# Attention of a two-layer token tower: value products in runs of eight, exponents in twelve buffers, maxima turned with 128 columns

## The reference

```python
# per sequence, 512 tokens, 12 heads of width 16
q, k, v = split(h_in @ w1)                       # h_in: normalised, scaled and masked rows of 192
s = softmax(q @ k.T / sqrt(16))                  # 512 x 512 per head
attn = s @ v                                     # 512 x 16 per head
out = concat(gelu(mlp part), attn) @ w2 + b2
```

## Time and profile before

| | before |
|---|---|
| median of 3 runs | 2166.76 us (2166.21 to 2169.19) |
| span of the profiled execution, first to last instruction | 2137.2 us |
| median of the runs less that span | 29.6 us |
| TensorE busy | 1949.3 us, 91% |
| VectorE busy | 1140.4 us, 53% |
| ScalarE busy | 739.9 us, 35% |
| mean granted TensorE clock | 0.938 |
| first score to last score of the eight turns | 357.86 us to 898.84 us |

### The profile page before, as it was taken

How to read it: one execution, slowest core, us unless ns; L and a number is a source line. 1 busy time by engine, 2 the same in 40 slices (tenths; PEclk the granted TensorE clock), 3 DMA queues, 4 the chain that set the end, 5 groups by cost and what they waited for, 6 DMA issues and landing times. The chain is left out here.

```text
span 2137.2 us, 28059 instructions
## 1 busy us (share of the span) xinstructions
PE 1949.3 (91%) x10067; PEld 1227.5 (57%) x10075; DVE 1140.4 (53%) x2776; ACT 739.9 (35%) x1248; POOL 426.2 (20%) x567
## 2 busy tenths in 40 slices
PE   4998629999999999879999998799999999999997
PEld 2343523344444544445666665465558888888886
DVE  5798567676667665456877785347322222222221
ACT  1434102544555455544556553121111111111111
POOL 5200111120222021111111111100551222222222
PEclk9988558999999999978999999699999999999999
DMA  2610002111111111000000000200222322122321
GB/s 63 223 50 0 0 18 81 53 52 53 45 53 53 52 45 52 1 31 6 6 6 6 11 6 1 100 1 1 77 95 61 69 60 59 32 62 61 69 38 18
DMA packets 68748, 94.75 MB, mean 44 GB/s; under 512 B 15386, under 2 KB 57662, under 8 KB 66337
## 3 DMA queue, kind: packets, MB, share of 16 engines
q1 hardware_dynamic: 52482, 77.19, 11.2%
q0 software_dynamic: 16128, 15.76, 4.3%
HBM read 54.96 MB, written 39.47 MB: 44 GB/s over the span
## 5 line engine op out<-in xcount | busy, mean ns | idle before, releaser
L1020 DVE TENSOR_REDUCE row_max<-c_ps_m 128x1 f32<-128x512 f32 x384 | 253.1, 686 | 113.8 <-PE c_ps_m L1190 108.5
L1368 ACT ACTIVATE e<-c_ps_s 128x512 f32<-128x512 f32 x384 | 216.5, 596 | 222.2 <-PE c_ps_s L1206 221.5
L2667 DVE TENSOR_TENSOR e_f<-e_ps_u,e_gate 128x512 f32<-128x512 f32 x120 | 83.0, 692 | 271.2 <-ACT e_gate L2949 179.1
L2468 POOL DMA_INDIRECT out<-m_o,m_row_of x80 | 125.7, 1571 | 282.0 <-issue 252.9
L2884 PE MATMUL e_ps_o<-m_w,e_f 128*128 128x192 f32 x960 | 162.6, 326 | 0.9 <-DVE e_f L2667 0.9
L1190 PE MATMUL c_ps_m<-c_kT,qT 96*128 96x512 bf16 x384 | 150.4, 398 | 10.7 <-DVE row_max L1020 10.0
L2884 PEld LDWEIGHTS e_ps_o<-m_w,e_f 128*128 128x128 f32 x960 | 158.1, 190 | 3.3 <-DVE e_f L2667 1.3
L1206 PE MATMUL c_ps_s<-qT,c_kT 97*128 97x512 bf16 x384 | 145.2, 389 | 12.7 <-ACT e L1368 5.3
L2949 ACT ACTIVATE e_gate<-e_ps_g 128x512 f32<-128x512 f32 x120 | 71.6, 597 | 242.3 <-PE e_ps_g L2858 162.3
L2852 PE MATMUL e_ps_g<-m_xT,m_w 128*128 128x256 f32 x480 | 129.6, 392 | 1.0 <-DVE h L2499 1.0
L2852 PE MATMUL e_ps_u<-m_xT,m_w 128*128 128x256 f32 x480 | 123.2, 379 | 0.0
(11 more groups left out here) (458 smaller groups left out, 3725.2 us busy)
## 6 DMA issues: line engine op xcount, KB each, us to landing
dealt<-x SPq DMA_DIRECT2D x8, 1290.0 KB, 15.1
m_x<-dealt SPq DMA_DIRECT2D x40, 258.0 KB, 2.7
spread<-parts SPq DMA_DIRECT2D x24, 384.0 KB, 2.3
qT<-spread SPq DMA_DIRECT2D x144, 64.0 KB, 2.4
c_kT<-spread SPq DMA_DIRECT2D x144, 64.0 KB, 2.5
m_w<-in_w13e SPq DMA_DIRECT2D x8, 1152.0 KB, 5.2
m_w<-in_w2e SPq DMA_DIRECT2D x8, 576.0 KB, 6.2
out<-h SPq DMA_DIRECT2D x8, 384.0 KB, 4.6
```

Source lines behind the costliest of these rows:

```text
L1020: dve.tensor_reduce(row_max[:, n // J, n % J:n % J + 1], ps_m[:, n % 2, :], AX_X, ALU.max)\
L1368: act.activation(e[:, n % LIVE_E, :], ps_s[:, n % 2, :], ACT.Exp, scale=QSCALE).then_inc(e_ready, 1)
L2468: pool.indirect_dma_start(out=out_rows, out_offset=bass.IndirectOffsetOnAxis(ap=row_of[:, n % 2, r:r + 1], axis=0), in_=o[:, n % 2, r, :], ...
L2667: dve.tensor_tensor(fe[:, n % 2, 2 * i:2 * i + 2, :], ps_ue[:, q % 2], gate_e[:, q % 2], ALU.mult)\
```

## The change

Two groups are weighed in one run, in steps 9, 17, 25, 33, 41 and (the last two) behind the first MLP tile of `between`; the exponents have 12 buffers, so that eight of them can wait while four are written. `neg_max` has 128 columns per group, 16 filled and 112 zero, and the turned maxima are a 128 x 128 matmul; its first 16 rows are read as before. `xaT` moves into memory of a weight that is no longer needed, to make room.

```diff
-LIVE_E = 8
+LIVE_E = 12
...
-        neg_max = sb("neg_max", [P, HEADS, J])
+        neg_max = sb("neg_max", [P, G3, P])
...
-        xaT = sb("xaT", [CH, 2, T])
+        xaT = moe.w2_other[0:CH, :, :].rearrange("p m c -> p (m c)")[:, 0:2 * T].rearrange("p (c t) -> p c t", c=2)
...
-                dve.tensor_scalar(neg_max[:, 4 * g:4 * g + 4, :], row_max[:, 4 * g:4 * g + 4, :], -1.0, None,
-                                  ALU.mult).then_inc(mx_ready, 1)
+                dve.tensor_scalar(neg_max[:, g, 0:GS].rearrange("p (h j) -> p h j", j=J), row_max[:, 4 * g:4 * g + 4, :],
+                                  -1.0, None, ALU.mult).then_inc(mx_ready, 1)
...
+            dve.memset(neg_max[:, :, GS:P], 0.0)
...
-                pe.transpose(bank(key)[0:4 * J, 0:P], neg_max[:, 4 * g:4 * g + 4, :], kit.ident[:, :])\
-                  .then_inc(w_psum, 1)
+                pe.transpose(bank(key)[:, 0:P], neg_max[:, g, :], kit.ident[:, :]).then_inc(w_psum, 1)
...
                 mlp_tile(t, 0)
+                weigh(t - 1, G3 * J - 2)
                 weigh(t - 1, G3 * J - 1)
...
-                    if n % 4 == 1 and n > 4:
+                    if n % 8 == 1 and n > 8:
+                        weigh(t, n // 4 - 2)
                         weigh(t, n // 4 - 1)
...
+            weigh(B - 1, G3 * J - 2)
             weigh(B - 1, G3 * J - 1)
...
-                if n % 4 == 0 and t * G3 * J + n // 4 >= 2:
-                    act.wait_ge(av_done, t * G3 * J + n // 4 - 1)
+                if n % 4 == 0 and t * G3 * J + n // 4 >= LIVE_E // 4:
+                    act.wait_ge(av_done, t * G3 * J + n // 4 - LIVE_E // 4 + 1)
```

## The result

The change takes 2189.07 us (4 runs, 2186.2 to 2191.03) against 2166.49 us for before: ratio 1.0097, 95% interval 1.0069 to 1.0124. Before itself had medians of 2166.49, 2182.64, 2176.24 and 2178.52 us in the four comparisons, so a time is only set against the before of its own comparison.

A forecast was written before the change was run, and what follows sets the result against it. TensorE was taken to bound most of a turn, VectorE or ScalarE two stretches (steps 13 to 17, 28 to 33). Moved weighs +8.2 and clock +3.1 gave +11.3 us: 2148.5 span plus 29.6, 2178.0 us, range 2163 to 2188.

The forecast's parts named there:

- the covers: Weighs of steps 13 and 29 hid in TensorE's waits; moving them adds 0.99 us (steps 10 to 17) and 0.96 (26 to 33).
- the walk: Step-by-step delays from moved weighs, net of savings: +1.25 us a turn in turns 1 to 5, +8.2 us over all turns.
- the clock: Sparser stretch before step 17 drops the clock in all seven turns, not five: 2 x 1.6 = +3.1 us, bounds none to 13.
- the run: Two groups weighed in one run take 2.00 us, not 2.18; 0.187 saved per pair, 9.0 us at most over 48 pairs.
- the signs I named: Right: S18 some 0.6 us later, `values` behind step 33 1.2 later; wrong: M17 more than 0.5 earlier.
- Turn 7: Last turn, without M: only the last run and the first two gain, -0.4 us.
- The third rival: More clock falls, in steps 28 to 33 and turn 7: eight more of 1.6 us, 2191 us; chance 0.12.
- 2148.5 of span: Forecast profiled span of the whole kernel: 2137.2 + 11.3 us, with 29.6 us added around it for the time.
- Wide transposes, buffers, memset, `xaT`: Side costs taken as nothing; the turned maxima's longer weight loads 1.2 us at most, taken as 0.
- that TensorE limits everywhere: Rival: covers reappear as slack, so 9.0 us come off, 2157.8 us; chance 0.13.
- that a second group pays its entry again: Rival: the second group of a run costs 1.09 us, so 9.0 are not saved, 2187 us; chance 0.05.
- That covers are half of the walk: Rival: new waits are 1.2 us a turn and the clock keeps five falls, +0.6 us, 2167.4 us; chance 0.17.

The follow-up runs named there:

- the change with five fillers: The change plus five unread matmuls a turn, three ahead of S16 and two behind it; attention 539.55 us, no fall begins in attention.
- before with six: The kernel before plus six unread matmuls a turn, four ahead of S16, two between S16 and M16; attention 533.42 us, ratio 0.9977.
- the profile again: The kernel before, unchanged, profiled once more: 2185.02 us, span 2183.3 us.
- the two kernels that undo parts of the change: The change with every group weighed in its old step, ratio to before 1.0005; the change with maxima turned as 16 columns, ratio 1.0069.
- the uncovered pairs: The change with pairs only in steps 17 and 33, all other groups in their old steps; attention 558.6 us.
- two covered pairs: The change with pairs only in steps 9 and 25, all other groups in their old steps; ratio to before 0.9970, attention 539.33 us.
- its two-pair version: Pairs only in steps 9 and 25, plus six unread matmuls a turn; attention 529.67 and 529.41 us, ratios to before 0.9982 and 0.9970.

## Why the prediction was right in sign and short in size

Taking the clock out on both sides (the change with five fillers, 539.55; before with six, 533.42) splits attention's 16.16 us: **6.1 us** without falls, and falls that cost 557.13 - 539.55 = 17.6 us in the change and 540.97 - 533.42 = 7.6 us before, **10.0 us** more. The direction and the covers were foreseen; the walk was 2.1 us too long and the clock 6.9 us too short, so the two errors partly cancel in attention's 16.2 for 11.3, which is luck.

- *The walk of the moved weighs*, 8.2 forecast, 6.1 measured. For a middle turn without falls, by the starts of the scores, the change with five fillers against before with six:

| stretch | walk | measured |
|---|---|---|
| S0 to S10 | -0.18 | -0.34 |
| S10 to S18 | +0.81 | +0.78 |
| S18 to S26 | -0.18 | -0.33 |
| S26 to S34 | +0.79 | +0.74 |
| S34 to S42 | -0.27 | -0.34 |
| S42 to the next S0 | +0.28 | +0.24 |
| sum | +1.25 | +0.75 |

  Both covers that I named were there, of the size I gave them to 0.05. The mis-sized term is the run: from the M before to the next start two groups take 2.17 us where I had 2.21 (the second adds 0.86, the lower bound, and not 0.91), a saving of 0.23 a pair. That alone is 0.25 of the 0.5 a turn. S0 to S10 and S18 to S26 gave a further 0.10 each: a group that leaves step 5 or 21 also frees the output product behind it, a term that I left out. Of the signs I named, S18 came 0.44 us later for 0.6, `values` 0.85 for 1.2, and M17 0.42 us earlier, near the 0.5 that would have spoken against me. Turn 0: +2.4 for 1.8 forecast. Turn 6: 0.0 for +0.5. Turn 7: 0.0 for -0.4; its last run won 0.5 and two others 0.3 each, but the pair of step 17 lost 0.9 there too, which the term left out, and the rest 0.3.
- *The clock*, 3.1 forecast, 10.0 measured: the step that failed. I counted falls, one a turn of 1.6 us, and let turns 2 and 4 join (2 x 1.6 is 3.2, not 3.1). All seven turns did get one around step 17. But in turns 2, 4 and 6 the clock is low twice as long (6.8 us in place of 3.4), turn 0 has a second fall at step 25, and turn 7 has two where before has none. Turn by turn, against the filled kernels, a single fall in a middle turn costs 1.3 to 1.4 us (before 1.6) and a double one 2.4. So of the 10.0 us more, turns 1 to 6 make 5.0, turn 0 2.0 and turn 7 3.0. The third rival had turn 7 right, which the forecast had not; its other place, steps 28 to 33, shows no fall in turns 1 to 6. Its 16 us of falls are about as far from the 10.0 as the forecast's 3.1. The 0.94 that I read as the fall of turn 0 was only half that fall; the other half is the low stretch that ends 4 us into attention.
- *Around the span*: the sum was set against the median with 29.6 us around the profiled span. In the profile again there are 1.7. The rest fits an execution whose routed stage was short: 248.7 us, where the twelve other profiles have 281 to 301. The difference forecast is not touched, but "2148.5 of span" was, by 36 us.
- *Wide transposes, buffers, memset, `xaT`* at nothing: shown by the two kernels that undo parts of the change. The load of 128 columns is 141 ns, as the row of the other transposes said.
- *Rivals*: that TensorE limits everywhere fell with the uncovered pairs (attention 558.6, not 538); that a second group pays its entry again fell with the 1.85 us run. That covers are half of the walk fell with 10.23 and 7.76 us. (The chance of slower was given as 0.68; its three parts add up to 0.70.)

## To carry to other kernels

Before joining work into longer runs, ask for each piece what it stood under: a piece that filled a wait was free, and moved behind the wait it costs its full length, however much the join saves (here 0.74 to 0.86 us lost per pair that stood under a wait, 0.34 won per pair that did not). The sparse stretch here cost twice, once as waiting and once as a lower clock for the dense work behind it; a few matmuls that nobody reads, put into the wait, brought 7.6 us of attention back, but the stretches behind have to be looked at too. And compare stages before whole spans: one stage here differs by 50 us between executions, while attention and the two other stages behind the first score repeat to 0.3 us in the same kernel.

## What the runs showed of the hardware

- In a run of column tiles (a pass is four records that start together) the first pass takes 0.45 us to the next, later ones 0.43 (0.454, 0.429, 0.429 in turn 0 of the change), the last 0.55 to the next start. The extra at entry and exit is paid once per run, 0.23 us saved per join. A 192-column product right behind a run has its successor 0.27 us behind it, in place of 0.17.
- Five matmuls a turn that nobody reads, 1.1 us of work at 0.22 each, in the waits ahead of S16 and M16, made the difference between no fall and ten falls to 1.2 GHz in attention, each 3.4 or 6.8 us long.
- Falls can come at the same place of every turn: with two covered pairs each of turns 1 to 6 has one, and each of these turns lasts 71.67 or 71.68 us.
- With attention free of falls, before and its two-pair version get a 10.2 us fall behind attention that the plain kernel does not have (470.6 to 470.8 against 466.5 us for that stage, in three profiles). The change, free of falls, gets 3.4 us.
